# A software-pipelined layer on one core: the order of its segments, its pipeline stages and its PSUM banks are all chosen anew

## What is computed

```
x = x + 0.5 * ffn(layernorm(x))      # sublayer 1
x = x + attn(layernorm(x))           # sublayer 2
x = x + 0.5 * ffn(layernorm(x))      # sublayer 3, same weights as 1

ffn(x):  x_prev = x shifted by one token
         xr, xk = mu_r*x + (1-mu_r)*x_prev,  mu_k*x + (1-mu_k)*x_prev
         return sigmoid(xr @ W_r) * (square(relu(xk @ W_k)) @ W_v)

attn(x): q, k, v = silu(dwconv4(x @ Wq.T)), ...          # 16 heads of 16
         q, k    = l2norm(q) / 4, l2norm(k)
         beta    = sigmoid(x @ Wb.T);  g = -exp(A_log) * softplus(x @ Wa.T + dt_bias)
         for each token t, each head:                     # state S is 16x16
             S = S * exp(g_t);  dv = (v_t - k_t S) * beta_t
             S = S + outer(k_t, dv);  o_t = q_t S
         return (rmsnorm(o) * norm_w * silu(x @ Wg.T)) @ Wo.T
```

## Time and profile before

| | us |
|---|---|
| runs of the kernel: median (lowest to highest of 3) | 1981.98 (1980.61 to 1982.77) |
| the profiled execution, its own time | 1983.11 |
| the profiled execution, span of the trace | 1981.2 |
| PE busy in the span | 1810.8 (91%) |
| DVE busy | 1596.2 (81%) |
| ACT busy | 1034.8 (52%) |
| POOL busy | 412.9 (21%) |
| chain of work that ended last | PE 77%, DVE 10%, issue 9%, ACT 1% |

### The profile page before, as it was taken

One profiled execution on the slowest core, in us unless ns is written; L12 is line 12 of the kernel. 1 busy time (PEld: TensorE's weight loads), 2 busy tenths in 40 slices (PEclk: granted clock), 3 DMA queues, 4 the chain that ended last, 5 costly groups with the idle time before them and its releaser, 6 DMA issues.

```text
span 1981.2 us, 102019 instructions
## 1 busy us (share of the span) xinstructions
PE 1810.8 (91%) x45376; PEld 1517.9 (77%) x45376; DVE 1596.2 (81%) x4326; ACT 1034.8 (52%) x1999; POOL 412.9 (21%) x325
## 2 busy tenths in 40 slices
PE   3778999999999999999999999999999999998886
PEld 2667887878788787878778887878887788787765
DVE  2767898889889888888888888898888889887641
ACT  3545555555555545555555555555555556554322
POOL 0211122222212222222122222122122221221200
PEclk8978999999999999999999999999999999998766
DMA  3000000000000000000000000000000000000000
GB/s 102 1 3 4 14 14 4 14 14 14 14 14 14 9 9 14 14 14 14 14 9 9 14 14 14 14 14 13 4 14 14 14 9 9 9 4 9 8 8 11
DMA packets 21445, 26.24 MB, mean 13 GB/s; under 512 B 2192, under 2 KB 20752, under 8 KB 21008
## 3 DMA queue, kind: packets, MB, share of 16 engines
q1 hardware_dynamic: 21008, 19.73, 3.1%
HBM read 11.33 MB, written 8.39 MB: 10 GB/s over the span
## 4 chain that ended last, share of the span: by engine, by line
PE 77%; DVE 10%; issue 9%; ACT 1%; POOL 0%; DVEq 0%; ACTq 0%; POOLq 0%
PE ps L234 36%; PE ps L216 15%; PE ps L225 9%; PE ps L209 4%; DVE CV L1087 3%; PE ps L402 2%; PE ps L356 2%; PE ps L202 2%; PE ps L560 2%; PE ps L570 2%; PE ps L579 1%; PE ps L372 1%; DVE XR L1364 1%; DVE eg L1344 1%; PE ps L457 1%
## 5 line engine op out<-in xcount | busy, mean ns | idle before, releaser
L1087 DVE SCALAR_TENSOR_TENSOR CV<-ps,cw,CV 128x256 f32<-128x256 f32 x576 | 250.5, 477 | 8.6 <-ACT CV L853 1.8
L234 PE MATMUL ps<-QE,S 64*64 64x16 f32 x4096 | 251.3, 209 | 1.0 <-ACT S L654 1.0
L234 PEld LDWEIGHTS ps<-QE,S 64*64 64x64 f32 x4096 | 209.0, 138 | 55.7 <-issue 54.2
L234 PE MATMUL ps<-WP,V 64*64 64x16 f32 x4096 | 248.9, 208 | 0.0
L234 PEld LDWEIGHTS ps<-WP,V 64*64 64x64 f32 x4096 | 210.0, 138 | 0.0
L234 PE MATMUL ps<-WP,KD 64*64 64x48 f32 x4096 | 147.6, 228 | 25.3 <-issue 23.9
L234 PEld LDWEIGHTS ps<-WP,KD 64*64 64x64 f32 x4096 | 137.5, 143 | 35.2 <-issue 33.8
L988 POOL TENSOR_TENSOR XK<-XK 128x512 f32<-128x512 f32 x32 | 33.5, 1048 | 607.8 <-ACT XK L827 607.8
L1102 DVE TENSOR_TENSOR prod<-A,TZ 128x30 f32<-128x30 f32 (+7 forms) x480 | 140.5, 293 | 13.2
L216 PE MATMUL ps<-w_r_ffn,XR 128*128 128x256 f32 x512 | 139.6, 421 | 9.1 <-DVE XR L1076 6.6
L234 PE MATMUL ps<-KQI,K 64*64 64x48 f32 x4096 | 144.2, 223 | 1.1 <-issue 1.0
(11 more groups left out here) (156 smaller groups left out, 4049.9 us busy)
## 6 DMA issues: line engine op xcount, KB each, us to landing
X<-in_x SPq DMA_DIRECT2D x32, 256.0 KB, 2.7
out_x<-X SPq DMA_DIRECT2D x32, 256.0 KB, 2.1
w_r_ffn<-in_wT_r_ffn SPq DMA_DIRECT2D x1, 256.0 KB, 2.8
w_k_ffn<-in_wT_k_ffn SPq DMA_DIRECT2D x1, 256.0 KB, 3.0
w_v_ffn<-in_wT_v_ffn SPq DMA_DIRECT2D x1, 256.0 KB, 3.8
w_q<-in_wT_q SPq DMA_DIRECT2D x1, 256.0 KB, 4.3
w_k<-in_wT_k SPq DMA_DIRECT2D x1, 256.0 KB, 4.8
w_v<-in_wT_v SPq DMA_DIRECT2D x1, 256.0 KB, 5.0
```

The costliest lines, as they stand in the source:

```text
L234: last = mm(ps[rows, o:o + n], stat[rows, pk].rearrange("p s c -> p (s c)"), mov[rows], **flags)
L1087: last = stt(d4[:, m], src, cw[:, i, m, tap:tap + 1], d4[:, m], ALU.mult, ALU.add)
```

## The change

All instructions, their shapes and their data stay. What is chosen anew is the position of every segment in the four lists, its lag in steps, and its PSUM bank; the waits follow from these. `NX` goes from 8 to 9 and the loops run one step more. ACT switches between its two tables of functions four times a step where it did so twice. The core of the diff (PE, ACT and the rest of DVE are changed in the same manner; two of the bank changes are shown):

```diff
-NX, NGS, NVT = 8, 4, 3
+NX, NGS, NVT = 9, 4, 3
@@ sync
-            for step in range(0, GROUPS + 6):
+            for step in range(0, GROUPS + 7):
                 on(load, step + 1)
-                on(store, step - 6)
+                on(store, step - 7)
@@ tensor
             def d_product0(g):
...
-                    last = pairs(5 * BANK + i * 3 * C, 3 * C, KD4, pk, WP[g % 2][:, pk], start=True, stop=True)
+                    last = pairs(4 * BANK + i * 3 * C, 3 * C, KD4, pk, WP[g % 2][:, pk], start=True, stop=True)
             def turn3(g):
                 pe.wait_ge(s["xn3"], g + 1)
-                pe.wait_ge(s["eq"], min(g + 3, GROUPS))
-                if g >= GROUPS - 2:
-                    pe.wait_ge(s["x2"], g + 1)
-                turn(2, XN[2], s["xt3_ps"])
+                pe.wait_ge(s["x2"], g + 1)
+                turn(5, XN[2], s["xt3_ps"])
@@ scalar, the end of a step
-                on(soft_ln, c)
-                on(norm2, b)
-                on(gates_wide, c)
-                on(yt, b)
+                on(norm2, b)
+                on(rstd1, a)
+                on(norm1, a)
+                on(xt1, a)
+                on(exp_q, c)
+                on(yt, b)
+                on(k_slots, c)
+                on(exp_d, c)
+                on(rstd3, e)
+                on(tap_q, b)
@@ gpsimd
-            for step in range(0, GROUPS + 6):
-                c, d, e, f, g = step - 2, step - 3, step - 4, step - 5, step - 6
-                on(g_ident, e)
-                on(b_diag, e)
-                on(square1, c)
-                on(square3, g)
-                on(gate_norm, f)
-                on(q_decayed, e)
-                on(stat1, d)
-                on(t_start, d)
-                on(e_mask, d)
-                on(g_diag, d)
+            for step in range(0, GROUPS + 7):
+                d, e, g, h = step - 3, step - 4, step - 6, step - 7
+                on(square3, h)
+                on(square1, d)
+                on(stat1, e)
+                on(gate_norm, g)
+                on(g_diag, e)
+                on(t_start, e)
+                on(g_ident, e)
+                on(q_decayed, e)
+                on(e_mask, e)
+                on(b_diag, e)
```

More of the change, by code:

```diff
@@ new lines, in turn3, with gate @@
+            def turn3(g):
+                pe.wait_ge(s["xn3"], g + 1)
+                pe.wait_ge(s["x2"], g + 1)
+                turn(5, XN[2], s["xt3_ps"])
+            def gate(g):
+                pe.wait_ge(s["yt"], g + 1)
+                pe.wait_ge(s["cq"], g + 1)
+                pe.wait_ge(s["z"], g + 1)
+                for m in range(M):
+                    for k in range(M):
+                        o = 3 * BANK + m * HB
+                        last = mm(ps[:, o:o + HB], w["g"][:, k, m * P:(m + 1) * P], YT[:, k, :, CT:], start=(k == 0), stop=(k == M - 1))
+                last.then_inc(s["g_ps"], 1)
@@ L408, in ffn1_r @@
                     pe.wait_ge(s["th1"], g)
[L409 to L421, removed]
+                if g >= 2:
+                    pe.wait_ge(s["ea"], g - 1)
@@ L610, in _ @@
+                on(gram0, c)
                 on(chain, d, 0)
-                on(decay_sums, c)
+                on(gram1, c)
+                on(turn3, e)
+                on(chain, d, 1)
+                on(gate, b)
+                on(chain, d, 2)
+                on(q_squares, b)
+                on(gram2, c)
+                on(chain, d, 3)
+                on(k_proj, b)
+                on(chain, d, 4)
+                on(gram3, c)
+                on(chain, d, 5)
+                on(ffn3_k, e)
@@ L612, in _ @@
+                on(chain, d, 6)
                 on(ffn1_r, a)
[L613 to L615 removed]
+                on(chain, d, 7)
                 on(ffn1_k, a)
[L617 to L625 removed]
@@ L662, in rstd1, with norm2 @@
+            def norm2(g):
+                act.wait_ge(s["nm2"], g + 1)
+                if g:
+                    act.wait_ge(s["yt_ps"], g)
+                for b in range(B):
+                    last = af(XN[1][:, b * H:(b + 1) * H], X[g % NX][:, b, :], ACT.Identity, bias=nmr[:, 1, b:b + 1], scale=rstd[:, 1, b:b + 1])
+                last.then_inc(s["xn2"], 1)
             def rstd1(g):
@@ L1540, in _ @@
[L1540 to L1554 removed]
+                on(gates_in, c)
+                on(conv_q, c)
@@ new lines, in _ @@
+                on(chain, e, 0)
+                on(gram0, d)
+                on(chain, e, 1)
+                on(gram1, d)
+                on(chain, e, 2)
+                on(soft_neg, c)
+                on(mix_k3, f)
+                on(gram2, d)
+                on(soft_one, c)
+                on(chain, e, 3)
+                on(mix_r3, f)
+                on(chain, e, 4)
+                on(b_reduce, d)
+                on(gram3, d)
+                on(chain, e, 5)
+                on(a_turn, d)
```

1340 lines of the change are left out of this document (639 added, 701 removed).

## The result

| | before | after |
|---|---|---|
| runs of the kernel: median (lowest to highest) | 1982.38 (1980.61 to 1983.04) | 2027.44 (2013.81 to 2039.35) |
| the profiled execution, its own time | 1983.11 | 2025.72 |
| its span | 1981.2 | 2023.9 |

The ratio of the medians is 1.023, with an interval of 1.016 to 1.029: the changed kernel is slower, on the side forecast and by somewhat over half of it (2058 was predicted, 2020 to 2105 for the likeliest case, 1975 to 2105 in all).

A forecast was written before the change was run, and what follows sets the result against it. PE was taken to bound the kernel. A step: +2.4 - 0.5 + 0.2 + 0.3 = +2.4 us; 31 steps +74, with filling +76, so 2058 us; range 1975 to 2105, likeliest case 2020 to 2105.

The forecast's parts named there:

- likeliest case: The mix of sublayer 1 collides with POOL's row and PE waits; 1.2 to 3.9 us a step, chance 0.66.
- signs: Steps of 59.9 us, PE waiting over 2 us for `SA`, mix instructions of 1.5 to 2.4 us, `turn3`'s wait gone or merged.
- First term: Mix of sublayer 1: POOL's instructions block DVE for 4.5 us, so PE waits 2.4 us at the chain's product 1.
- Third term: PE's clock falls after a further wait of over 2 us; +0.3 us a step, bounds 0 to 1.2.
- what a new order can gain: On PE, the 0.47 us wait before `turn3` goes and the 1.8 us issue idle stays; -0.5 us a step.
- second term: PE's `t_product0` waits for `t_turn`, behind DVE's solve that POOL's squares block; +0.2 us a step.
- the two ends of the kernel: Filling and draining: `turn2` of the first group stands behind `turn1` of the second; some 2 us more in all.
- Table loads of ACT: ACT's two further table loads a step stand where ACT waits, so they cost 0.
- The mix gets through: Mix delayed by under 1.4 us, PE waits for nothing new, `turn3`'s 0.47 us go; 1970 us, chance 0.16.
- no change: A mix delay of 1.5 to 2.2 us costs what `turn3` gave back; 1980 to 1988 us, chance 0.08.
- PE's own dense row: A second 1.8 us gap in PE's row, mix costing nothing; +1.7 us a step, 2036 us, chance 0.10.
- The order's gain is elsewhere: Durations counted wrongly, PE late at several places; +3.5 us a step, 2090 us, counted into the first case's upper end.

The follow-up runs named there:

- kernel 1: The changed kernel with one wait more: POOL's `g_diag` waits for the end of the mix of sublayer 1; 1943.15 us, ratio to before 0.980.
- kernels 1, 3, 4 and 5: Kernel 1; changed kernel, `g_diag` and `g_ident` cut small (1957.33 us); kernel before, `g_ident` behind `soft_neg` (1986.12) or `shift3` (1955.41); changed kernel, `g_ident` alone cut (1984.85).
- experiment 2: The changed kernel with ACT's loop two steps shorter, leaving out steps that held only table loads; 2015.09 us, ratio to before 1.016.
- experiment 6: Kernel 1 with the mix's two `XK` instructions written once more (1976.08 us) or three times more (2095.84 us); base repeated at 1942.88 us.

## Why the prediction was right, and where a size was off

**The place.** The mix of sublayer 1 meets POOL's row, the chain's first copy is late, PE waits at product 1, and the time is given back when POOL waits (kernel 1): as predicted. The Trainium skill (SBUF — State Buffer, section SBUF: two separate sides) has the pair of ports as an exclusive lock, first come, first served; kernels 1, 3, 4 and 5 agree, down to the case in which the block moved on to `eg4`, 0.29 to 1.61 us. Two of the signs that I gave came out smaller than said: steps of 58.50 us, not 59.9, and a wait for `SA` of 1.46, not over 2.

**First term, the collision: +4.5 us of mix, +2.4 of wait.** The mix lengthened by 2.75. I had three blocks of POOL's full lengths, by `g_diag`, `g_ident` and `q_decayed`, and none by `t_start`. Against kernel 1's 0.48 an instruction they are 0.90 by `g_diag`, 0.35 by `t_start` and 1.59 by `g_ident`, each less than the time of POOL's instruction. `q_decayed` waits for `g_ident`'s end (0.26 us) and starts at 1022.10, when the last mix instruction is already running. From `turn1`'s start to the copy's end it took 13.4 us (14.2 predicted), PE was there at 12.0 (11.15 or 12.4 predicted), and the wait is 1.46 us a step.

**Third term, the clock behind the wait: +0.3, bounds 0 to 1.2.** `gate` lost 0.6 us a step. Collision and clock together were put at 2.7 and cost 2.62 by kernel 1: the waits for `SA` (1.46 - 0.10) and for `turn3` (0.29), `gate` (0.6), and 0.4 that I can't itemise. That the sum agrees is luck: the wait for `SA` was put at 2.4 and is 1.36 more than in kernel 1, the clock at 0.3 and is 0.6, and `turn3`'s wait was to be gone. The prediction's "2 us into `wo`" is a slip of reading, too: the earlier trace rows are the first 2 us of `wo`.

**The term that failed in its size: what a new order can gain, -0.5.** By kernel 1 it was 1.61, nearly all of it in three parts. The wait for `turn3` gives 0.47, as said (in the changed kernel itself 0.29 of it is back). The issue idle, which I "leave as it is", went from 1.80 to 1.32 us (27.3 us in 20.6 steps). In the window of 1153 us this line is 36.1 to 41.3 us in all four kernels with the old order and 23.2 to 27.3 in all with the new. No run shows what this idle is, so it does not speak against what the prediction sets it beside. And `wo` runs at full clock, 0.6 us a step: I had quoted its 3.23 us and counted only a new fall of the clock, not the end of the old one. With 1.6 in place of 0.5 the sum is +1.3 a step where +2.4 stood, and +1.01 was measured.

In the whole time this is 31 x 1.1 = 34 us less, against the 31 between 2058 and 2027. The terms that were off besides nearly cancel: the 0.2 of the second term did not come, and the two ends of the kernel cost 3.1 + 8.3 = 11.4 us where 2 stood. There is luck in that: +1.01 a step lies below the 1.2 that the likeliest case had as its lower bound, and with ends of 2 us the time would have been some 2016, outside that case's 2020 to 2105; it is inside it by the ends, which I had not foreseen.

**Second term, `t_product0` after `t_turn`: +0.2.** No wait of PE for `T` is in its list; nothing to see of it.

**Table loads of ACT: 0.** In the steady steps none of PE's waits leads to one, though no run tests it by itself. At the end of the kernel they are what ends last: 6.5 us (experiment 2), while the filling took 3.1 us where 2 stood.

**The rivals.** "The mix gets through" needed a delay under 1.4 us; it was 2.75, and "no change" one of 1.5 to 2.2. With kernel 1's wait the time is even under that rival's 1970, since the order is worth more than I thought. "PE's own dense row": issue idle fell instead. "The order's gain is elsewhere" wanted PE late at several places; it is late at two, both behind the mix. A comparison of the two orders, each with its collision moved off the path, is 1942.88 to 1955.41: the new order is better by 12.5 us (the runs of the two overlap; the steps, 56.01 and 56.97, differ by 1.0), and one meeting of two engines costs it 85 (2028.3 to 1942.88; by the steps, 31 x 2.62 = 81).

## What to carry to other kernels

A planner that counts durations measured alone does not see that an instruction of POOL can stop one of DVE; put POOL's long instructions, by a semaphore if need be, beside DVE work that reads PSUM, and after moving one look at the next two-input instruction in the list. Price a wait of the bounding engine with the clock that falls behind it, and price in the same way a wait that goes. Where a loop is lengthened for its pipeline, let each engine's loop end at its own last segment.

## What the runs showed of the hardware that I had not expected

- A block can move on instead of going: with `soft_neg` out of the way (1616 to 224 ns), `eg4` took it over (0.29 to 1.61 us), and the kernel gained nothing.
- The clock falls in some steps only, behind the same wait: in the kernel after `gate` takes 1.99 us behind 1.49 us of idle at 1029.02, and 3.78 at 1205.19; it is slow in 8 of the window's 20 steps. `gate`'s mean grows with the wait (table in experiment 6); with 2.8 us of waits a step it is slow in nearly all steps (647 ns). What decides in a single step isn't shown.
- The idle for which the profile shows nothing ("issue") depends on the order: 1.80 us a step before, 1.22 after, 1.32 with kernel 1, on the same instructions.
